# A graph network on one core: two message buffers in place of four, and the adjacency products moved behind the messages

## The reference

```
edge_index = stack([src, dst])
x = layernorm(x + L0(x))   # sum over edges of weight * (x @ kernel)[edge's row], + bias
x = layernorm(x + L1(x))   # 8 bases of 128x128, mixed by the edge's type (64 types), summed per target
x = layernorm(x + L2(x))   # one of two 128x128 products by the edge's type (2 types), summed, + self, relu
x = layernorm(x + L3(x))   # two graph convolutions with degrees
```

```
support  = inp @ kernel
messages = edge_val[:, None] * support[edge_col]
output   = segment_sum(messages, edge_row, num_segments=6250) + bias
```

## Time and profile before

| | |
|---|---|
| median of 3 runs | 5841.46 us (5829.03 to 5850.34) |
| the profiled execution's own time | 5841.46 us |
| its span | 5839.8 us |
| first stage, first to last L630 | 84.6 to 1812.5 us |
| GpSimd busy over the span | 3066.2 us |
| TensorE busy over the span | 3723.5 us |
| VectorE busy | 2170.8 us |
| ScalarE busy | 1028.2 us |

### The profile page before, as it was taken

One profiled execution on the slowest core, in us unless ns is written; L12 is line 12 of the kernel. 1 busy time (PEld: TensorE's weight loads), 2 busy tenths in 40 slices (PEclk: granted clock), 3 DMA queues, 4 the chain that ended last, 5 costly groups with the idle time before them and its releaser, 6 DMA issues.

```text
span 5839.8 us, 90251 instructions
## 1 busy us (share of the span) xinstructions
PE 3723.5 (64%) x20675; PEld 2509.5 (43%) x20676; DVE 2170.8 (37%) x8525; ACT 1028.2 (18%) x2045; POOL 3066.2 (53%) x2549
## 2 busy tenths in 40 slices
PE   4666666666662544545454444444445999989998
PEld 3333333333331333434343343344334666656664
DVE  5665666666664333333333122222222111111122
ACT  3444444444443000000000000000000000000000
POOL 3777777778777666666665666566654000000000
PEclk7877777778775666667676555555555999989999
DMA  8676666666767111111111111111112666666664
GB/s 249 151 165 146 159 152 147 160 150 150 164 148 169 45 48 46 51 47 51 47 51 41 43 45 44 44 45 45 45 44 87 205 205 205 206 196 206 204 206 141
DMA packets 382424, 693.89 MB, mean 119 GB/s; under 512 B 56824, under 2 KB 233889, under 8 KB 371568
## 3 DMA queue, kind: packets, MB, share of 16 engines
q1 hardware_dynamic: 190180, 373.66, 21.4%
q0 software_dynamic: 176272, 185.39, 17.8%
q10 hardware_dynamic: 15804, 133.26, 6.0%
HBM read 474.67 MB, written 220.82 MB: 119 GB/s over the span
## 4 chain that ended last, share of the span: by engine, by line
PE 26%; DVEq 9%; another core or an unknown queue 9%; issue 8%; DVE 5%; ACT 0%; DMA 0%; POOL 0%; POOLq 0%; ACTq 0%
PE bank L1026 21%; DVEq L1272 6%; PE bank L928 3%; DVE alpha L1263 1%; DVE acc L1265 1%; DVE arena L1265 1%; PE bank L893 1%; DVEq L1265 1%; DVE S L1241 1%; DVEq L1254 1%; DVE idx_ring L1157 0%; PE bank L925 0%; DVEq L1241 0%; PE bank L895 0%
## 5 line engine op out<-in xcount | busy, mean ns | idle before, releaser
L590 POOL DMA_INDIRECT rows<-t,idx_ring x1664 | 1647.1, 990 | 945.3 <-issue 468.6
L928 PE MATMUL bank<-S,rows 128*128 128x192 f32 (+1 forms) x3328 | 926.5, 422 | 704.7 <-DVE arena L1265 422.2
L928 PEld LDWEIGHTS bank<-S,rows 128*128 128x128 f32 x3328 | 774.8, 293 | 839.7 <-DVE arena L1265 470.3
L1092 PE MATMUL bank<-arena 128*128 128x384 bf16 (+1 forms) x2496 | 652.9, 420 | 549.2 <-DVE arena L1584 527.9
L1026 PE MATMUL bank<-alpha,arena 128*128 128x384 bf16 x5460 | 902.9, 327 | 0.0
L630 POOL DMA_INDIRECT sums<-stage,idx_ring x416 | 673.0, 1618 | 244.2 <-DMA sums<-rows,idx_ring 128.5
L630 POOL DMA_INDIRECT sums<-rows,idx_ring x416 | 683.4, 1643 | 145.2 <-issue 109.4
L1026 PEld LDWEIGHTS bank<-alpha,arena 128*128 128x128 bf16 x5460 | 535.8, 98 | 354.3 <-issue 6.2
L1092 PEld LDWEIGHTS bank<-arena 128*128 128x128 bf16 x2496 | 254.0, 118 | 888.0 <-issue 729.4
L925 PE MATMUL bank<-S,ones 128*1 128x24 f32 x1664 | 132.4, 210 | 720.5 <-DVE acc L1265 612.0
L1482 DVE TENSOR_TENSOR acc<-acc,bank 128x24 f32 x832 | 149.7, 180 | 803.4 <-issue 484.0
(11 more groups left out here) (154 smaller groups left out, 3599.6 us busy)
## 6 DMA issues: line engine op xcount, KB each, us to landing
alpha<-adj SPq DMA_DIRECT2D x260, 672.0 KB, 4.3
adj<-xcur ACTq DMA_DIRECT2D x26, 2352.0 KB
adj<-acc ACTq DMA_DIRECT2D x26, 2352.0 KB
arena<-src_row SPq DMA_DIRECT2D x104, 512.0 KB
rows<-adj SPq DMA_DIRECT2D x52, 672.0 KB, 4.3
S<-adj SPq DMA_DIRECT2D x52, 672.0 KB, 4.3
arena<-type SPq DMA_DIRECT2D x52, 512.0 KB
rows<-t,idx_ring POOLq DMA_INDIRECT x1664
```

The lines of the kernel that those rows point to most:

```text
L590: nc.gpsimd.indirect_dma_start(out=rows[:, k, t, :], out_offset=None, in_=tables[p], in_offset=bass.IndirectOffsetOnAxis(ap=idx_ring[:, k, ...
L928: last = nc.tensor.matmul(bank[k % 2][:, 0:width], rows[:, k, t, :], of_group[:, t, 0:width], start=t == 0, stop=t == GT - 1)
L1092: last = nc.tensor.matmul(bank[bk][:, 0:(hb - ha) * W], lo_hot[n * GT + t], hw_hot[n * GT + t][:, ha * W:hb * W], start=t == 0, stop=t == ...
```

## The change

Three things are changed, all in the first stage.

1. The message buffers are two (`msg[k % 2]`, in the tile `rows`) in place of four (the other two were in `stage`), and `keep_rows` of step g waits for GpSimd's fourth DMA of step g - 1 in place of step g - 3.
2. TensorE multiplies the window of the next step and the messages of this step first, and builds this step's adjacency behind them.
3. ScalarE copies in the same order: next window, message, then the six adjacency copies. The wait for the last body's store moves behind the first message copy.

```diff
+        msg = [rows4[:, s, :, :] for s in range(2)]
...
-        msg = [rows4[:, s, :, :] for s in range(2)] + [a[:, :].rearrange("p (t f) -> p t f", t=FT) for a in stage]
-        assert len(msg) == FSTEPS
...
                             out=sums_t[t], out_offset=bass.IndirectOffsetOnAxis(ap=idx4[:, k, t:t + 1], axis=0),
-                            in_=msg[k][:, t, :], in_offset=None, compute_op=ALU.add).then_inc(scattered[t], 16)
+                            in_=msg[k % 2][:, t, :], in_offset=None, compute_op=ALU.add).then_inc(scattered[t], 16)
...
             def keep_rows(i, k):
                 act.wait_ge(messages, i * FSTEPS + (k + 5))
-                act.wait_ge(scatter_through, i * FSTEPS + (k + 1))
-                nc.scalar.activation(msg[k].rearrange("p t f -> p (t f)"), bank[4 + k % 2][:, :],
+                act.wait_ge(scatter_through, i * FSTEPS + (k + 3))
+                nc.scalar.activation(msg[k % 2].rearrange("p t f -> p (t f)"), bank[4 + k % 2][:, :],
                                      ACT.Copy).then_inc(msg_kept, 1)
...
                     keep_window(i, 0)
-                    act.wait_ge(adj_stored[u], c * 16 + 16)
                     for k in range(FSTEPS):
-                        keep_adjacency(i, u, k)
                         if k < FSTEPS - 1:
                             keep_window(i, k + 1)
                         keep_rows(i, k)
+                        if k == 0:
+                            act.wait_ge(adj_stored[u], c * 16 + 16)
+                        keep_adjacency(i, u, k)
...
                 window_by_edge(i, 0)
-                for k in range(FSTEPS):
-                    build_adjacency(i, k)
-                    if k < FSTEPS - 1:
-                        window_by_edge(i, k + 1)
+                for k in range(FSTEPS - 1):
+                    window_by_edge(i, k + 1)
                     if k == 1:
                         body_weights(i)
                     rows_to_add(i, k)
+                    build_adjacency(i, k)
+                rows_to_add(i, FSTEPS - 1)
+                build_adjacency(i, FSTEPS - 1)
```

## The result

The changed kernel takes 6063.83 us in the median of four runs (6058.60 to 6067.31), against 5840.05 us before: 1.0383 of it, 95% interval 1.0362 to 1.0404, or 224 us more. The forecast was 5955 us with a range from 5835 to 6080. Direction and mechanism were right; the size was half.

A forecast was written before the change was run, and what follows sets the result against it. GpSimd's DMA chain was taken to bound the first stage, 33.23 us a body; the new ring would take 35.4. 2.2 us over 52 bodies gave +114 on 5841, so 5955 us, range 5835 to 6080.

The forecast's parts named there:

- GpSimd bounds the first stage: First stage, kernel before: GpSimd's DMA chain sets the pace, 33.23 us a body, 30.9 unstalled; the message producers have slack.
- The new order closes a ring on TensorE and VectorE: First stage: window waits for wS, wS for one-hots, one-hots for TensorE; a turn of 8.31 us, in all +114 us.
- TensorE's run, 5.7 us: In each turn, window, messages and adjacency matmuls at a mixed clock take 5.7 us, after an idle gap of 2.61 us.
- the forecast's full clock: A turn with TensorE at full clock: a run of 4.57 us, 7.18 us in all, a body 30.9 us.
- every run starts at the low clock: Rival, chance 0.12: each gap costs TensorE the full clock, run 6.42 us, body 38.3 us, +264 us, 6105 us.
- Four turns a body: First stage: one turn is one step, so a body takes 4 x 8.31 + 2.2 = 35.4 us.
- Two buffers at nothing: Message copy: the freed buffer is announced some 2 us into a step, the copy hidden with about 4.7 us to spare.
- ScalarE's order at nothing: First stage: ScalarE's copies, 3.8 us a step, lie beside TensorE's run; new order and moved store wait cost nothing.
- the tail at 0: Last body: the store is over before the tables are read again; 0 taken, from -1 to +3 us.
- the sign of 10 us behind the last scatter: After the first stage: a difference of more than 10 us behind the last scatter would show the prediction wrong.
- The stalls shrink: Rival, chance 0.10: the later store takes away half of GpSimd's 122 us of stalls, -61 us, 5781 us.
- Signs named ahead: Changed profile: L629's steps 8.9 us, GpSimd waiting 60 us or more for message copies, TensorE gaps of about 2.6 us.

The follow-up runs named there:

- e5: The kernel before with a body's adjacency store cut in three pieces, issued in the next body: 0.9805 of the kernel before.
- e3: The changed kernel with VectorE making hits, sel and wS of the next step ahead of this step's one-hot tiles: 1.0174 of the kernel before.
- e8: The changed kernel with nothing but the store in three pieces: 1.0398 of the kernel before.
- e4: The changed kernel with filler matmuls of constant tiles in TensorE's idle gaps: 1.0142 of the kernel before.
- e2: The kernel before, old order, with two message buffers and the new wait: 1.0238 of the kernel before.
- e6: e2 with the store issued ahead of the body's last message copy: 1.0024 of the kernel before.
- e1: The changed kernel, new order, with four message buffers and the old wait back: 1.0378 of the kernel before.
- e10: The kernel before, old order, with two message buffers and the store in three pieces: 0.9863 of the kernel before.

## Why the prediction was right in its way and short by half

- **GpSimd bounds the first stage.** Right for the kernel before. e5 takes most of the stalls away, and the stage falls to 1606 us from first to last start, the sum of DMAs and 0.30 us pauses that the prediction worked out.
- **The new order closes a ring on TensorE and VectorE.** Right (changed kernel, e3, e8). The gap of a whole turn is 2.52 us where 2.61 was worked out.
- **TensorE's run, 5.7 us.** This term failed: 7.46 us. The choice "between the mean's 5.4 and the 5.9 of the gap it is nearest to" was too low, and so was even the upper bound of 6.4, "window and messages at 1.2 GHz ..., adjacency at full clock again". One gap of 2.88 us in the kernel before was taken as a measure for gaps that come in every turn. In the trace nearly the whole run is at 1.2 GHz, the adjacency too (3.6 us for 2.4). e4 confirms it from the other side: with the gaps filled the turn has the length of the forecast's full clock. The rival "every run starts at the low clock", 6105 us, was nearer to the mechanism than the forecast, and even it let the clock rise too soon. The Trainium skill, in "TensorE: Matmul & The Clock Gate", section "HAM oscillation — how this bites in real kernels", describes bursts that begin at the low clock after every wait, in a kernel whose waits are longer than 2.52 us; this trace agrees on the bursts, with 0.54 granted in the run, and shows the clock at 1.00 in the gap, which the section does not describe. The prediction's sum also has a slip: with 6.2 us for the run a body is 4 x (2.61 + 6.2) + 2.2 = 37.4 us, not 37.0, and the time 6060 us, not 6037.
- **Four turns a body.** This was wrong too, in the other direction. 4 x (2.61 + 7.46) + 2.2 = 42.5 us would be a body; measured are 1950.6 / 52 = 37.5. At a body's end the window of the next body stands behind the adjacency, as before, so that messages and adjacency of step 3 need no new wS. In the trace they follow step 2's run without a gap and at the full clock (2.42 us for the adjacency at 1043.38). Behind them and the next window comes the gap of 5.11 us, in which VectorE is busy nearly throughout (4.96 us in 1084.57 to 1089.67, one body later). Only the turns from 1052.02 to 1062.01 and on to 1072.60 are whole ones, 9.99 and 10.59 us; the other two steps share the remaining 37.5 - 20.6 = 16.9. The run was short by 1.8 us and two of four turns were too many: the errors cancel in part, 37.5 against the 35.4 forecast, 2.1 x 52 = 109 us. That the measured time lies inside the range owes something to luck: with the run as measured and four turns the sum would have come to about 6320 us.
- **Two buffers at nothing.** Wrong as a general statement, right for this kernel. The semaphore does come early and the copy is in time (2.3 us of waits in e2). What the prediction missed under this head is what is queued behind the waiting copy: a store of 2,352 KB, and with it most of e2's 139 us (e2, e6). In the changed kernel this is hidden, because the ring is longer (e1, e8).
- **ScalarE's order at nothing, the tail at 0.** No run changed ScalarE's order alone, since with TensorE's old order the two engines would wait for each other in a circle. The store did not move nearer to the loads either: in the changed kernel the type load follows it by 4.5 us in the median, before by 3.8. The tail is right as far as the medians tell: the first stage alone makes up their difference. Taken by its letter, the sign of 10 us behind the last scatter came in the profiled execution (24 us).
- **"The stalls shrink", 0.10.** The mechanism exists and is worth 2% (e5), but this change doesn't reach it.
- **Signs named ahead.** GpSimd's waits for the message copy came (248 us), gaps ended by wS, VectorE's indices no longer waited for GpSimd, and eight window matmuls took more than 1.05 us: the median of one is 417 ns, where it was 273 before.

```profile
L1071 PE MATMUL bank<-shared,wS x1664: 272/417/421, 67.6 to 2012.0; 128*24 128x128 f32 x185
```

GpSimd's steps took 9.38 us, not 8.9. That the waits for landing DMAs "should fall" came in a small measure, 150 to 129 us, so that many of GpSimd's waits did still end by them.

What stays open: why GpSimd's DMAs take some 20 us more with two buffers in the old order (e10), and how much of the ring's loss ScalarE's order has, if any.

## What to carry to other kernels

When an order changes, draw the ring: follow one semaphore round through all engines until it comes back to its start, and count the turns at the loop's seams too, since the last step of a body may be another one. When TensorE gets a regular gap of some 2.5 us in every turn, as here, reckon its whole run at 1.2 GHz too until a trace shows otherwise; filling the gap with harmless matmuls can be worth more than it costs. When a wait is added, look past the waiting instruction to the DMA issues behind it: it is their place against other transfers that may cost.

## What the runs showed of the hardware

- The granted clock can run in opposite phase to the work: 0.54 and 0.56 in two runs of TensorE, 1.00 and 0.99 in the gaps behind them. That this holds in most turns is seen in the window matmuls, with a median of 417 ns. Filler matmuls of 3.8 us once and of 2.0 us twice a body brought the mean of the stage from 0.70 to 0.90 (e4).
- GpSimd's queue runs ahead of its engine by more than one DMA: an increment that is written ahead of the fourth DMA of a step released VectorE 3.8 us before that DMA began.
- A store of 2,352 KB that starts within a microsecond of two loads of 512 KB goes with about 5.0 us of pauses in GpSimd's scatter chain a time (e2; the pauses above 0.4 us among its next ten DMAs, added up, in the mean of 46 bodies). 3.8 us ahead of the loads it goes with about 2.8 us (before), and in thirds spread over a body with hardly anything (23 us of waits in the whole stage in e5).
- The same kernel took 5415 us on one occasion and 5840 us on another. The chip's number on record is the same for both (15, e1 to e4 and e5 to e8), so whether they are two chips or two states of one is open. GpSimd's idle time before the gathers of the later passes is 534 us in e5's trace (first kind) and 945 us in that of the kernel before (second kind), and the gathers themselves take 0.99 us in both. Why was not looked into.
